# Gated attention scores kept in rows: masking by a TensorE bias, and one joint transposition of both attentions' probabilities

## The chip, the cores and the metric

The kernel runs on one core of a Trainium2 chip. The metric is the device time of one execution in microseconds (us), as the median of several executions. TensorE (PE in the rows) multiplies and transposes into PSUM; VectorE (DVE), ScalarE (ACT) and GpSimd (POOL) do the elementwise work; SyncE (SP) issues the DMAs.

## The reference, cut to what matters

One transformer layer over x of 2 x 1024 rows of 512. Its attention has 32 query heads over 8 key heads (4 query heads share a key head), head size 128, and is the mean of two attentions: a gated linear one (a scan with a decaying state) and a softmax over a sliding window of 64 positions.

```python
def step(S, x):
    q_t, k_t, v_t, g_t = x
    S = S * jnp.exp(g_t)[..., None] + k_t[..., None] * v_t[..., None, :]
    return (S, jnp.einsum('bhk,bhkv->bhv', q_t, S))
...
o_lin = gla_scan(softmax(q), softmax(k), v, log_sigmoid(g) / GATE_NORM)   # g = k before the softmax
y = sliding_window_attn(rope(q), rope(k), v)    # W = 64: the block of 64 and the one before it, masked, softmax
o_ = 0.5 * y + 0.5 * o_lin
x = x + _layernorm(_L0_attn_ref(_layernorm(x), ...))
x = x + _layernorm(_L0_ffn_ref(_layernorm(x), ...))   # NF4 quantised weights, silu(gate) * up, w3
```

## The kernel before

The attention part goes through 128 turns: 8 key heads times 16 tiles of 128 positions. A turn handles one tile for one key head, hence 4 query heads, hence tensors of 128 x 512. Turns are unrolled by four, as a step of a hardware loop (32 steps); the position in the step is `t.p`, 0 to 3. Every engine runs its own `turn(t)`, whose stages work on tile `t`, on the one before (`l1`), two before (`l2`) and three before (`l3`), and waits on counters (`wait_tile`) for the others. The order of work on each engine is that in which its `turn` is written. Nothing is reordered by a scheduler.

The gated attention of a tile is done in chunks. `gla_scores` (TensorE, tile `l2`) multiplies the scaled queries `qtT` (which VectorE writes last in a turn, in `gla_q`, semaphore `qt_d`) with the scaled keys `ktT` into PSUM bank X1, with keys on the partitions. `mask_gla` (VectorE) multiplies X1 by a 0/1 causal mask into `am`. The softmax probabilities of the window, `pr`, have queries on the partitions; `probabilities` (TensorE) transposes them into the same bank X1 once `am` is out, and `add_gla` (VectorE) adds X1 and `am` into `pa`. `output` multiplies `pa` with the values.

Names that the prediction uses, with their engine and line: `qtT` (VectorE L587, the last work of a turn but for the dequantisation in turn 0), `am` (VectorE L615), `kt` (VectorE L579, the keys' softmax times decay), `gh`, `kneg` and `gl` (VectorE L554, L555, L560: logarithm of the decay in two halves, functions `log_decay` and `low_decay`), `su` and `sr` (VectorE L627, L638: the state), `pa` (VectorE L621), `pmx`/`npm` (VectorE L601, L604: maxima of the window's scores, function `p_max`, which waits for `sc_done` of `scores` on TensorE, L883 and L891), `rp` (VectorE L610, reciprocal of the softmax sums), `qrT` (ScalarE L428, a copy out of PSUM that `scores` needs). Beside the attention, VectorE and GpSimd dequantise the second part's weights: VectorE writes fifteen terms `f_s` (L676) for each step, in portions of 2, 4, 5 and 4 over the four turns, and GpSimd adds them up in `f_acc` (L343) one turn later, so in portions of 4 (turn 0), 1 (turn 1), 4 (turn 2) and 5 (turn 3).

In this text "turn 2" is a turn with `t.p` of 2, and likewise turn 0, 1 and 3.

Of the kernel before, what the change touches and what calls it, by code (L numbers as in the profile page):

```python
# [34 lines left out]
P = 128  # L35
# [106 lines left out]
def attention(nc, sem, bank, rows, xh, xl, ident, stats, x_rows, wq_v, wk_v, wv_v, wo_v, wf_v, wf_p, dq_v, dq_p,  # L142
              cosc, sinc, winmask, causal, cumsum, identc, keepc):

    with ExitStack() as ctx:
        def sb(name, shape, dt=F32):
# [10 lines left out]
        cau = sb("cau", [P, 512])  # L157
# [13 lines left out]
        qtT = sb("qtT", [P, 2, GRP, 2, WIN])  # L171
        pr = sb("pr", [P, 2, 512])
        am = sb("am", [P, 512])
# [46 lines left out]
            rp_d am_d pa_d su_d em_d sr_d acc_d qrope_p krope_p qn_p pn_p  # L220
# [22 lines left out]
        def _(sp):  # L243
# [33 lines left out]
            for dst, src in ((cos[:], cosc), (sin[:], sinc), (f_s[:, 0:2, :], winmask), (cau[:], causal), (cum[:], cumsum),  # L277
                             (keep[:], keepc)):
                sp.dma_start(dst, src).then_inc(s["consts"], 16)
# [104 lines left out]
        def _(act):  # L384
# [56 lines left out]

            def copy_ktT(t):
# [34 lines left out]
            def turn(t):  # L477
                l1, l3 = t.back(1), t.back(3)
                if l3.real():
                    copy_o(l3)  # L480
                if l1.real():
                    q_exps(l1)
                    decays(l1)
                if t.real():
                    k_exps(t)
                    nf4_abs(t)
                if l1.real():
                    copy_qrT(l1)
# [35 lines left out]
        def _(dve):  # L524
# [57 lines left out]
            def gla_q(t):  # L582
# [107 lines left out]
            def turn(t):  # L690
# [7 lines left out]
                if l2.real():  # L698
                    mask_gla(l2)
# [96 lines left out]
            nc.vector.tensor_copy(win[:], f_s[:, 0:2, :]).then_inc(s["z_id"], 1)  # L796
            nc.vector.tensor_copy(cumh[:], cum[:]).then_inc(s["z_id"], 1)
# [620 lines left out]
```

## Time and profile before

| | |
|---|---|
| median of 3 runs | 2118.87 us (2117.91 to 2120.97) |
| span of the profiled execution | 2121.1 us |
| busy share of the span: TensorE | 89% |
| VectorE | 81% |
| ScalarE | 53% |
| GpSimd | 61% |
| one step (4 turns) in the middle of the attention part | 51.55 us |

For the profiled execution the profile gives its span, and no other time; the span stands 2.2 us above the median of the runs, which is 0.1%. The attention part takes about the first 1730 us. The shares of the whole span mix it with the last part, in which TensorE works nearly alone, so the rows further down come from the steady stretch in the middle.

### The profile page before, as it was taken

The numbers are of one execution on the slowest core, as the hardware profiler recorded it, in microseconds if no ns is written. First come the engines' busy times: TensorE is split into PE (matmuls) and PEld (weight loads), VectorE is DVE, ScalarE is ACT, GpSimd is POOL, SyncE is SP. The second block draws the span as 40 slices with busy tenths as digits, with TensorE's granted clock in tenths as the row PEclk, the third lists the DMA queues.
The fourth block names the chain that finished last, engine by engine and source line by source line (L and its number), as shares of the span: only waits on it lengthen the run. The fifth ranks groups of instructions, "written<-read, shape, count | busy, mean of one in ns | idle before, by whom it ended". The sixth has DMA issues, their size and how long they took to land. (4 is left out here: it accounts for less than half of the span.)

```text
span 2121.1 us, 41545 instructions
## 1 busy us (share of the span) xinstructions
PE 1893.0 (89%) x10676; PEld 1170.7 (55%) x10676; DVE 1724.4 (81%) x4335; ACT 1122.9 (53%) x4514; POOL 1292.9 (61%) x1189
## 2 busy tenths in 40 slices
PE   3799999998899999999999999998999869999998
PEld 2455555555555555555555555555555535544443
DVE  6899999999999999999999999999999964412022
ACT  6555555555555555555555555555555545512121
POOL 4777777767776677777777777777777724112111
PEclk8999999999999999999999999999999979999999
DMA  5000000000000000000000000000000033100000
GB/s 177 22 23 22 22 22 22 22 24 26 27 22 22 22 22 22 22 22 22 22 22 22 22 22 24 28 22 22 22 22 22 15 110 100 36 21 20 0 20 20
DMA packets 47051, 63.85 MB, mean 30 GB/s; under 512 B 5232, under 2 KB 20080, under 8 KB 47024
## 3 DMA queue, kind: packets, MB, share of 16 engines
q1 hardware_dynamic: 47024, 63.52, 9.3%
q8 instruction: 13, 0.21, 0.0%
q14 instruction: 14, 0.11, 0.0%
HBM read 50.86 MB, written 12.65 MB: 30 GB/s over the span
## 5 line engine op out<-in xcount | busy, mean ns | idle before, releaser
L343 POOL TENSOR_TENSOR f_acc<-f_acc,f_s 128x512 f32<-128x512 f32 x416 | 552.6, 1328 | 26.1 <-POOL f_acc L343 0.5
L437 ACT ACTIVATE pr<-bank,npm 128x128 f32<-128x128 f32 x512 | 180.9, 366 | 402.1 <-DVE npm L604 402.1
L864 PE MATMUL bank<-wh,xh 128*128 (+1 forms) x1024 | 335.2, 327 | 4.0 <-POOL wl L331 4.0
L864 PE MATMUL bank<-wl,xh 128*128 (+1 forms) x1024 | 335.0, 327 | 0.0
L864 PE MATMUL bank<-wh,xl 128*128 (+1 forms) x1024 | 334.7, 327 | 0.0
L325 POOL TENSOR_TENSOR pr<-pr,rp 128x512 f32<-128x512 f32 x128 | 133.1, 1039 | 257.4 <-DVE rp L610 257.4
L409 ACT ACTIVATE qe<-bank,nqm 128x128 f32<-128x128 f32 x512 | 180.9, 365 | 189.2 <-DVE qs L536 189.2
L676 DVE TENSOR_SCALAR f_s<-f_nrm 128x512 f32<-128x512 f32 x480 | 243.1, 568 | 4.4
L1349 POOL TENSOR_TENSOR hl<-hf,hh 128x512 f16<-128x512 f32 (+1 forms) x44 | 50.8, 1154 | 288.2 <-ACT hh L1218 288.2
L307 POOL TENSOR_TENSOR qc<-qc,qs 128x512 f32<-128x512 f32 x128 | 162.7, 1271 | 75.9 <-DVE qs L536 75.6
L1287 DVE SCALAR_TENSOR_TENSOR hf<-bank,sg 128x512 f32<-128x512 f32 (+1 forms) x44 | 30.4, 690 | 218.4 <-PE bank L1137 206.8
L853 PE MATMUL bank<-wh,oT 128*128 (+1 forms) x512 | 194.3, 380 | 4.1 <-ACT oT L473 2.5
L853 PE MATMUL bank<-wl,oT 128*128 (+1 forms) x512 | 194.0, 379 | 0.0
L842 PE MATMUL bank<-qtT,ktT 128*128 128x512 f32 x256 | 137.5, 619 | 29.9 <-DVE qtT L587 29.9
L318 POOL TENSOR_TENSOR qe<-qe,rq 128x512 f32<-128x512 f32 x128 | 147.3, 1151 | 0.5 <-DVE rq L596 0.5
L1137 PE MATMUL bank<-xh,w12h 128*128 (+3 forms) x352 | 135.3, 384 | 2.6 <-DVE xl L1244 1.4
L864 PEld LDWEIGHTS bank<-wh,xl 128*128 (+1 forms) x1024 | 100.6, 98 | 67.1 <-issue 1.1
L864 PEld LDWEIGHTS bank<-wl,xh 128*128 (+1 forms) x1024 | 100.6, 98 | 66.6 <-issue 0.6
L891 PEld LDWEIGHTS bank<-krT,qrT 128*128 128x128 f32 x1024 | 135.0, 192 | 3.6
L891 PE MATMUL bank<-krT,qrT 128*128 128x128 f32 x1024 | 135.6, 275 | 0.0
L1137 PE MATMUL bank<-xl,w12h 128*128 (+3 forms) x352 | 135.4, 385 | 0.0
L1137 PE MATMUL bank<-xh,w12l 128*128 (+3 forms) x352 | 135.2, 384 | 0.0
(176 smaller groups left out, 5017.2 us busy)
## 6 DMA issues: line engine op xcount, KB each, us to landing
raw_qkv<-wq SPq DMA_DIRECT2D x36, 256.0 KB, 2.3
raw_o<-wo SPq DMA_DIRECT2D x36, 256.0 KB, 2.6
f_raw<-wf SPq DMA_DIRECT2D x33, 256.0 KB, 2.6
dequantised<-f_dq SPq DMA_DIRECT2D x32, 256.0 KB, 2.0
wt<-dequantised SPq DMA_DIRECT2D x31, 256.0 KB, 3.1
rows<-x SPq DMA_DIRECT2D x4, 1024.0 KB, 8.7
xr<-x SPq DMA_DIRECT2D x16, 256.0 KB, 5.2
out<-yo SPq DMA_DIRECT2D x16, 256.0 KB, 2.0
```

What stands on the lines that cost most here:

```text
L307: nc.gpsimd.tensor_tensor(qc[:, r, :], qc[:, r, :], qs[:, r, :], ALU.add).then_inc(s["qrope_p"], 1)
L318: nc.gpsimd.tensor_tensor(v, v, rq[:, r, :].unsqueeze(2).to_broadcast([P, GRP, P]), ALU.mult).then_inc(s["qn_p"], 1)
L325: nc.gpsimd.tensor_tensor(v, v, rp[:, r, :].unsqueeze(2).to_broadcast([P, GRP, P]), ALU.mult).then_inc(s["pn_p"], 1)
L343: nc.gpsimd.tensor_tensor(f_acc[:], f_acc[:], f_s[:, k % 8, :], ALU.add).then_inc(s["f_ad"], 1)
L409: last = nc.scalar.activation(qe[:, r, h * P:(h + 1) * P], PQ[:, h * P:(h + 1) * P], ACT.Exp, bias=nqm[:, r, h:h + 1], scale=1.0 / WSCALE, ...
L437: last = nc.scalar.activation(pr[:, r, j * P:(j + 1) * P], SC[:, j * P:(j + 1) * P], ACT.Exp, bias=npm[:, r, j:j + 1], scale=ATT_SCALE, ac ...
L676: nc.vector.tensor_scalar(f_s[:, k % 8, :], f_nrm[:], float(BOUND[k]), float(DELTA[k]), ALU.is_gt, ALU.mult).then_inc(s["f_sd"], 1)
L842: nc.tensor.matmul(X1[:], ktT[:, r, :], qtT[:, r].rearrange("p h b n -> p b h n"), start=True, stop=True).then_inc(s["at_done"], 1)
L853: last = nc.tensor.matmul(PW[:], oT[:, t.p % 2, h].rearrange("p b n -> p (b n)"), w[:, sl + h, QW + KVW:WW], start=(h == 0 and k == 0), st ...
L864: last = nc.tensor.matmul(dst, av, w[:, sl + c, lo:hi], start=(n == 0), stop=(n == 3 * NC - 1))
L891: last = nc.tensor.matmul(SC[:, j * P:(j + 1) * P], qrT[:, r, b, 2 * hp:2 * hp + 2, :].rearrange("p h n -> p (h n)"), keys, start=False, s ...
L1137: last = nc.tensor.matmul(dst[0:n, :], ww[:, d, off + c * P:off + c * P + n], x4, start=(k == 0), stop=(k == 3 * NC - 1))
```

## The change

Five things change at once.

1. `gla_scores` swaps its operands, so the gated scores come out with queries on the partitions, as `pr` has them. Instead of one product of 512 columns there are four (two of 64 key columns, two of 128). Ahead of them two bfloat16 products with the identity add a bias `cau`, 0 where a key is allowed and -3e38 where it isn't.
2. `mask_gla` and `add_gla` go. A new `merge` on VectorE takes the maximum of X1 and 0 and adds it to `pr`, in place, over 128 and then 256 columns. The 128 columns left of the 512 can hold no gated score.
3. `probabilities` transposes that sum, and ScalarE copies it out of X1 into `pa` (`copy_pa`).
4. On ScalarE `copy_qrT` moves ahead of `k_exps`. On VectorE `log_decay` moves from before `state` to behind `p_max`.
5. `qtT` is laid out by window block first, then head; the mask is converted to bfloat16 once at the start.

```diff
@@ scalar
+            def copy_pa(t):
+                wait_tile(act, s["pt_done"], t)
+                wait_tile(act, s["o_done"], t, 2)
+                nc.scalar.activation(pa[:, t.p % 2, :], X1[:], ACT.Copy).then_inc(s["pa_ev"], 1)
@@ scalar turn
                 if l1.real():
                     q_exps(l1)
                     decays(l1)
+                    copy_qrT(l1)
                 if t.real():
                     k_exps(t)
                     nf4_abs(t)
+                if l2.real():
+                    copy_pa(l2)
                 if l1.real():
-                    copy_qrT(l1)
                     p_exps(l1)
@@ vector
-            def mask_gla(t):
+            def merge(t):
+
                 wait_tile(dve, s["at_done"], t)
-                wait_tile(dve, s["pa_d"], t, 1)
-                nc.vector.tensor_tensor(am[:], X1[:], cau[:], ALU.mult).then_inc(s["am_d"], 1)
-
-            def add_gla(t):
-                wait_tile(dve, s["pt_done"], t)
-                wait_tile(dve, s["am_d"], t)
-                wait_tile(dve, s["o_done"], t, 2)
-                nc.vector.tensor_tensor(pa[:, t.p % 2, :], X1[:], am[:], ALU.add).then_inc(s["pa_d"], 1)
+                wait_tile(dve, s["pn_p"], t)
+                v = pr[:, t.p % 2, :]
+                half = lambda a: a.rearrange("p (h n) -> p h n", h=GRP)[:, 0:2, 0:WIN]
+                nc.vector.scalar_tensor_tensor(out=half(v), in0=half(X1[:]), scalar=0.0, in1=half(v),
+                                               op0=ALU.max, op1=ALU.add)
+                nc.vector.scalar_tensor_tensor(out=v[:, 2 * P:], in0=X1[:, 2 * P:], scalar=0.0, in1=v[:, 2 * P:],
+                                               op0=ALU.max, op1=ALU.add).then_inc(s["pm_d"], 1)
@@ vector turn
                 if l2.real():
-                    mask_gla(l2)
+                    merge(l2)
                 if l1.real():
                     gla_k(l1)
                 if l3.real():
                     add_out(l3)
-                if t.real():
-                    log_decay(t)
                 if l2.real():
                     state(l2)
-                    add_gla(l2)
                 if l1.real():
                     p_max(l1)
                 if t.real():
+                    log_decay(t)
                     low_decay(t)
@@ tensor, gla_scores
-                wait_tile(pe, s["pa_d"], t, 1)
-                nc.tensor.matmul(X1[:], ktT[:, r, :], qtT[:, r].rearrange("p h b n -> p b h n"),
-                                 start=True, stop=True).then_inc(s["at_done"], 1)
+                wait_tile(pe, s["pa_ev"], t, 1)
+                half = lambda a: a.rearrange("p (h n) -> p h n", h=GRP)[:, 0:2, 0:WIN]
+                nc.tensor.matmul(half(X1[:]), identb[:], half(cau[:]), start=True, stop=False)
+                nc.tensor.matmul(X1[:, 2 * P:], identb[:], cau[:, 2 * P:], start=False, stop=False)
+                for b in range(2):
+
+                    keys = (b + 1) * WIN
+                    for hp in range(2):
+                        j = 2 * b + hp
+                        last = nc.tensor.matmul(X1[:, j * P:j * P + keys],
+                                                qtT[:, r, b, 2 * hp:2 * hp + 2, :].rearrange("p h n -> p (h n)"),
+                                                ktT[:, r, 0:keys], start=False, stop=(j == 3))
+                last.then_inc(s["at_done"], 1)
@@ tensor, probabilities
-                wait_tile(pe, s["pn_p"], t)
-                wait_tile(pe, s["am_d"], t)
+                wait_tile(pe, s["pm_d"], t)
```

On VectorE, a turn from the masking to the last half of the decay stood so before (a name ahead of the arrow is what is written, "bank" is PSUM, `rows` the running output):

```order
L615 TENSOR_TENSOR am<-bank,cau 128x512 [waits s_pa_d,s_at_done]
L575 RECIPROCAL rks<-ksum 128x1 [waits s_ke_ev]
L579 SCALAR_TENSOR_TENSOR kt<-ke,rks,ked 128x128 [waits s_u_done,s_dec_ev,s_rks_d]
L646 TENSOR_TENSOR rows<-bank,rows 128x512 [waits s_wo_done,s_zeroed]
L554 TENSOR_TENSOR gh<-kneg,kabs 128x128 [waits s_small_done,s_kneg_d,s_l1_ev]
L555 TENSOR_TENSOR kneg<-kneg,kabs 128x128
L627 TENSOR_TENSOR su<-bank,sr 128x128 [waits s_u_done]
L638 TENSOR_SCALAR sr<-su,edT 128x128 [waits s_su_d,s_dec_ev]
L621 TENSOR_TENSOR pa<-bank,am 128x512 [waits s_am_d,s_pt_done]
L601 TENSOR_REDUCE pmx<-bank 128x4 [waits s_sc_done]
L604 TENSOR_SCALAR npm<-pmx 128x4 [waits s_pmx_d]
L560 TENSOR_TENSOR gl<-kneg,gh 128x128 [waits s_g_d]
```

and so in the changed kernel:

```order
L625 SCALAR_TENSOR_TENSOR pr<-bank,pr 128x2x64 [waits s_pn_p,s_at_done]
L627 SCALAR_TENSOR_TENSOR pr<-bank,pr 128x256
L581 RECIPROCAL rks<-ksum 128x1 [waits s_ke_ev]
L585 SCALAR_TENSOR_TENSOR kt<-ke,rks,ked 128x128 [waits s_u_done,s_dec_ev,s_rks_d]
L653 TENSOR_TENSOR rows<-bank,rows 128x512 [waits s_wo_done,s_zeroed]
L634 TENSOR_TENSOR su<-bank,sr 128x128 [waits s_u_done]
L645 TENSOR_SCALAR sr<-su,edT 128x128 [waits s_su_d,s_dec_ev]
L608 TENSOR_REDUCE pmx<-bank 128x4 [waits s_sc_done]
L611 TENSOR_SCALAR npm<-pmx 128x4 [waits s_pmx_d]
L560 TENSOR_TENSOR gh<-kneg,kabs 128x128 [waits s_small_done,s_kneg_d,s_l1_ev]
L561 TENSOR_TENSOR kneg<-kneg,kabs 128x128
L566 TENSOR_TENSOR gl<-kneg,gh 128x128 [waits s_g_d]
```

The 128 x 512 multiplication and addition are gone, two shorter operations stand at the head, and `gh` and `kneg`, which stood between `kt` and `su`, now stand directly ahead of `gl`, with the wait for TensorE's scores (`s_sc_done`) ahead of all three.

On ScalarE, the same turn's work from the copies of the rotated keys to the first exponentials of the window was, before:

```order
L420 ACTIVATE ked<-bank 128x128
L423 ACTIVATE edT<-bank 128x130 [waits s_sr_d,s_qt_d]
L391 ACTIVATE va<-bank 128x128 [waits s_o_done,s_krope_d,s_kv_done]
L392 ACTIVATE vm<-bank 64x128
L393 ACTIVATE vm<-bank 64x128
L396 ACTIVATE ke,ksum<-bank,nkm 128x128 [waits s_nkm_d]
L398 ACTIVATE kabs<-bank 128x128
L400 ACTIVATE kabs<-kabs 128x128 [waits s_kabs_ev]
L402 ACTIVATE kabs<-kabs 128x128 [waits s_e1_ev]
L428 ACTIVATE qrT<-bank 128x4x2x64 [waits s_sc_done,s_qrT_done]
L437 ACTIVATE pr,psm<-bank,npm 128x128 [waits s_pt_done,s_npm_d]
L437 ACTIVATE pr,psm<-bank,npm 128x128 x3
```

and is now:

```order
L419 ACTIVATE ked<-bank 128x128
L422 ACTIVATE edT<-bank 128x130 [waits s_sr_d,s_qt_d]
L427 ACTIVATE qrT<-bank 128x4x2x64 [waits s_sc_done,s_qrT_done]
L390 ACTIVATE va<-bank 128x128 [waits s_o_done,s_krope_d,s_kv_done]
L391 ACTIVATE vm<-bank 64x128
L392 ACTIVATE vm<-bank 64x128
L395 ACTIVATE ke,ksum<-bank,nkm 128x128 [waits s_nkm_d]
L397 ACTIVATE kabs<-bank 128x128
L399 ACTIVATE kabs<-kabs 128x128 [waits s_kabs_ev]
L401 ACTIVATE kabs<-kabs 128x128 [waits s_e1_ev]
L444 ACTIVATE pa<-bank 128x512 [waits s_pt_done]
L436 ACTIVATE pr,psm<-bank,npm 128x128 [waits s_pt_done,s_npm_d]
```

The copy `qrT` moved ahead of seven instructions, and the new copy `pa` stands between them and the exponentials.

On TensorE, the path from the gated scores to the scores of the window was, before (`bank<-qtT,ktT` are the gated scores, `bank<-ident,qc` and `bank<-ident,pr` transpositions, `bank<-krT,qrT` the scores of the window):

```order
L842 MATMUL bank<-qtT,ktT 128x512 [waits s_pa_d,s_ktT_ev,s_qt_d]
L834 MATMUL bank<-ident,qc 128x128 [waits s_qt_d,s_qrope_p]
L834 MATMUL bank<-ident,qc 128x128 x3
L908 MATMUL bank<-qtT,sr 128x512 [waits s_oT_ev,s_sr_d]
L911 MATMUL bank<-va,kt 128x128 [waits s_dec_ev]
L901 MATMUL bank<-ident,pr 128x128 [waits s_am_d,s_pn_p]
L901 MATMUL bank<-ident,pr 128x128 x3
```

and is now:

```order
L849 MATMUL bank<-cau,identb 128x2x64 [waits s_pa_ev,s_ktT_ev,s_qt_d]
L850 MATMUL bank<-cau,identb 128x256
L856 MATMUL bank<-ktT,qtT 128x64 x2
L856 MATMUL bank<-ktT,qtT 128x128 x2
L840 MATMUL bank<-ident,qc 128x128 [waits s_qt_d,s_qrope_p]
L840 MATMUL bank<-ident,qc 128x128 x3
L923 MATMUL bank<-qtT,sr 128x512 [waits s_oT_ev,s_sr_d]
L926 MATMUL bank<-va,kt 128x128 [waits s_dec_ev]
L916 MATMUL bank<-ident,pr 128x128 [waits s_pm_d]
L916 MATMUL bank<-ident,pr 128x128 x3
```

One product became six; the rest of the row keeps its order, and the transposition (`bank<-ident,pr`) waits for `merge` in place of `am` and the normalised `pr`.

## Rows read from the trace of the kernel before

**Rows 1.** The page's head: the span of the profiled execution.
```profile
span 2121.1 us, 41545 instructions
```

**Rows 2.** Stretch 400 to 600 us: busy PE, PEld, DVE, ACT, POOL; PE clock, DMA.
```profile
400.00:600.00 200.00, 181.12 (x1073) 118.16 (x1072) 190.05 (x483) 116.02 (x512) 143.50 (x132) 1.00 0.07 22
```

**Rows 3.** Timeline of VectorE in turn 2: start, us, instruction, idle before.
```profile
1002.53 0.68 DVE L587 TENSOR_TENSOR qtT<-bank,edT 128x512 f32<-128x512 f32 x1
...
1005.21 0.69 DVE L615 TENSOR_TENSOR am<-bank,cau 128x512 f32<-128x512 f32 x1 [0.85 <-PE bank L842]
...
1006.00 1.03 DVE L579 SCALAR_TENSOR_TENSOR kt<-ke,rks,ked 128x128 f32<-128x128 f32 x1
...
1007.55 0.82 DVE L554 TENSOR_TENSOR gh<-kneg,kabs 128x128 f16<-128x128 f32 x1
1008.30 0.28 DVE L555 TENSOR_TENSOR kneg<-kneg,kabs 128x128 f32<-128x128 f32 x1
...
1008.89 0.90 DVE L638 TENSOR_SCALAR sr<-su,edT 128x128 f32<-128x128 f32 x1
...
1010.31 0.67 DVE L601 TENSOR_REDUCE pmx<-bank 128x4 f32<-128x512 f32 x1
...
1011.10 0.28 DVE L560 TENSOR_TENSOR gl<-kneg,gh 128x128 f16<-128x128 f32 x1
1011.30 1.76 DVE L676 TENSOR_SCALAR f_s<-f_nrm 128x512 f32<-128x512 f32 x5
```

**Rows 4.** Timeline of GpSimd in turn 2: its four additions, then two alone.
```profile
1005.61 5.44 POOL L343 TENSOR_TENSOR f_acc<-f_acc,f_s 128x512 f32<-128x512 f32 x4
...
1006.96 1.27 POOL L343 TENSOR_TENSOR f_acc<-f_acc,f_s 128x512 f32<-128x512 f32 x1
...
1008.31 1.39 POOL L343 TENSOR_TENSOR f_acc<-f_acc,f_s 128x512 f32<-128x512 f32 x1
```

**Rows 5.** Timeline of VectorE and GpSimd in turn 3.
```profile
1015.47 0.68 DVE L587 TENSOR_TENSOR qtT<-bank,edT 128x512 f32<-128x512 f32 x1
...
1018.55 7.03 POOL L343 TENSOR_TENSOR f_acc<-f_acc,f_s 128x512 f32<-128x512 f32 x5
...
1022.95 3.58 DVE L676 TENSOR_SCALAR f_s<-f_nrm 128x512 f32<-128x512 f32 x4
```

**Rows 6.** Timeline of turn 0: the score path on TensorE, and what surrounds it.
```profile
1028.94 0.67 DVE L587 TENSOR_TENSOR qtT<-bank,edT 128x512 f32<-128x512 f32 x1
...
1029.67 1.12 PE L842 MATMUL bank<-qtT,ktT 128*128 128x512 f32 x2 [0.90 <-DVE qtT L587]
...
1032.15 0.60 PE L901 MATMUL bank<-ident,pr 128*128 128x128 f32 x4
...
1033.44 0.58 ACT L428 ACTIVATE qrT<-bank 128x512 f32<-128x512 f32 x1
...
1034.12 0.38 PE L883 MATMUL bank<-win,identb 128*128 128x512 bf16 x1 [1.37 <-issue]
...
1034.34 1.05 PE L891 MATMUL bank<-krT,qrT 128*128 128x128 f32 x8
...
1037.28 0.52 DVE L655 SCALAR_TENSOR_TENSOR f_safe<-f_max 128x8 f32 x1
...
1033.57 1.40 POOL L343 TENSOR_TENSOR f_acc<-f_acc,f_s 128x512 f32<-128x512 f32 x1
```

**Rows 7.** Timeline of turn 1: masking, the transposition, the last small subtraction.
```profile
1045.33 0.68 DVE L615 TENSOR_TENSOR am<-bank,cau 128x512 f32<-128x512 f32 x1
...
1046.16 0.63 PE L901 MATMUL bank<-ident,pr 128*128 128x128 f32 x4 [1.02 <-DVE am L615]
...
1049.91 0.28 DVE L560 TENSOR_TENSOR gl<-kneg,gh 128x128 f16<-128x128 f32 x1
```

**Rows 8.** Groups by line: count, busy us, mean ns, idle before and its cause.
```profile
L615 DVE TENSOR_TENSOR am<-bank,cau 128x512 f32<-128x512 f32 x128 | 88.1, 688 | 29.3 <-PE bank L842 27.1
...
L1287 DVE SCALAR_TENSOR_TENSOR hf<-bank,sg 128x512 f32<-128x512 f32 x40 | 27.6, 691 | 195.2 <-PE bank L1137 183.6 <-issue 11.5
```

More of the change, by code:

```diff
@@ L156, in attention @@
         identb = sb("identb", [P, P], BF16)
-        cau = sb("cau", [P, 512])
+        cau = sb("cau", [P, 512], BF16)
         cum = sb("cum", [P, 130])
@@ L170, in attention @@
         qrT = sb("qrT", [P, 2, 2, GRP, WIN])
-        qtT = sb("qtT", [P, 2, GRP, 2, WIN])
+        qtT = sb("qtT", [P, 2, 2, GRP, WIN])
         pr = sb("pr", [P, 2, 512])
-        am = sb("am", [P, 512])
         pa = sb("pa", [P, 2, 512])
@@ L276, in _ @@
             load_weights(1, 0, 1)
-            for dst, src in ((cos[:], cosc), (sin[:], sinc), (f_s[:, 0:2, :], winmask), (cau[:], causal), (cum[:], cumsum),
+            for dst, src in ((cos[:], cosc), (sin[:], sinc), (f_s[:, 0:2, :], winmask), (f_s[:, 2, :], causal), (cum[:], cumsum),
                              (keep[:], keepc)):
@@ L477, in turn @@
             def turn(t):
-                l1, l3 = t.back(1), t.back(3)
+                l1, l2, l3 = t.back(1), t.back(2), t.back(3)
                 if l3.real():
@@ L586, in gla_q @@
                 wait_tile(dve, s["o_done"], t, 2)
-                nc.vector.tensor_tensor(qtT[:, r].rearrange("p h b n -> p h (b n)"),
-                                        X0[:].rearrange("p (h n) -> p h n", h=GRP),
-                                        edT[:, r, 0:P].unsqueeze(1).to_broadcast([P, GRP, P]), ALU.mult)\
+                nc.vector.tensor_tensor(qtT[:, r].rearrange("p b h n -> p h b n"),
+                                        X0[:].rearrange("p (h b n) -> p h b n", h=GRP, b=2),
+                                        edT[:, r, 0:P].rearrange("p (b n) -> p b n", b=2).unsqueeze(1)
+                                        .to_broadcast([P, GRP, 2, WIN]), ALU.mult)\
                     .then_inc(s["qt_d"], 1)
@@ L796, in _ @@
             nc.vector.tensor_copy(win[:], f_s[:, 0:2, :]).then_inc(s["z_id"], 1)
+            nc.vector.tensor_copy(cau[:], f_s[:, 2, :]).then_inc(s["z_id"], 1)
             nc.vector.tensor_copy(cumh[:], cum[:]).then_inc(s["z_id"], 1)
             nc.vector.memset(krT[:], 0.0).then_inc(s["z_id"], 1)
-            dve.wait_ge(s["z_id"], 5)
+            dve.wait_ge(s["z_id"], 6)
             turns(dve, 3, turn)
@@ L814, in _ @@
             pe.wait_ge(s["consts"], 96)
-            pe.wait_ge(s["z_id"], 5)
+            pe.wait_ge(s["z_id"], 6)
             slot = lambda t: (t.i // NC) % 2 * NC
@@ L907, in inter_and_update @@
                 wait_tile(pe, s["oT_ev"], t, 1)
-                nc.tensor.matmul(PO[:], sr[:, r, :], qtT[:, r].rearrange("p h b n -> p b h n"), start=True, stop=False)
+                nc.tensor.matmul(PO[:], sr[:, r, :], qtT[:, r].rearrange("p b h n -> p (b h n)"), start=True, stop=False)
                 if t.back(-1).real():
@@ L925, in output @@
                 r = t.p % 2
-                wait_tile(pe, s["pa_d"], t)
+                wait_tile(pe, s["pa_ev"], t)
                 wait_tile(pe, s["v_ev"], t)
@@ L1383, in constants @@
     win = np.ascontiguousarray(win.reshape(P, 2, 512))
+    n = np.arange(P)[:, None] % WIN
+    cau = np.zeros((P, 2, 2, P), np.float32)
+    for b in range(2):
+        cau[:, b] = np.where(n + b * WIN >= slot, 0.0, -3e38)[:, None, :]
+    cau = np.ascontiguousarray(cau.reshape(P, 512))
     j = np.arange(P)[:, None]
     i = np.arange(P)[None, :]
-    cau = (j <= i).astype(np.float32).reshape(P, 2, 1, WIN)
-    cau = np.ascontiguousarray(np.broadcast_to(cau, (P, 2, GRP, WIN)).reshape(P, 512))
     mid = P // 2 - 1
```

2 lines of the change are left out of this document (1 added, 1 removed).

## The prediction

> **What bounds the kernel now.** The span is 2121.1 us, 2.2 us above the median of the runs [rows 1]. I read the stretches first, because the whole span mixes two kinds of work. In the steady 200 us of the attention part VectorE is busy for 190.05 us, TensorE for 181.12, GpSimd for 143.50 and ScalarE for 116.02, at a granted TensorE clock of 1.00, the 2.4 GHz level, and a DMA share of 0.07 [rows 2]. So VectorE is the bound, and TensorE is close behind. No transfer is in the way, and the change moves none but the mask's, once, at the start.
>
> But 190 us busy is not 190 us of work, and that decides this case. In the timeline of VectorE `gh` takes 0.82 us while the equally wide `kneg` right behind it takes 0.28 [rows 3]. `gh` ends at 1008.37, and an addition on GpSimd ends at 1008.23 (1006.96 + 1.27). `sr` takes 0.90 us and ends at 1009.79; the next addition ends at 1009.70 (1008.31 + 1.39) [rows 3, 4]. `kt`, 1.03 us, ends at 1007.03, beside the addition's end at about 1006.9. All three have no PSUM operand. `am`, which reads PSUM, lies over GpSimd's work just the same and has its usual 0.69 us in all turns [rows 3, 8]. I read this as a rule of the trace: a VectorE instruction whose tensors all lie in SBUF, issued while GpSimd runs one, is held until that one has ended. One that gets in ahead of GpSimd's next addition goes through (`kneg` starts at 1008.30, the addition at 1008.31, and that addition then lasts 1.39 us in place of 1.27). The additions come every 1.36 us or so with 0.08 us between them.
>
> The Trainium skill (GPSIMD Engine Reference, Key points) says that GpSimd shares its SBUF interfaces with VectorE and that they contend where VectorE has two SBUF inputs or is in a two-port mode. The trace agrees: 0.82 us against 0.28.
>
> **The simple sum.** Per turn VectorE loses `am` and `pa`, two operations of 128 x 512 with a mean of 0.688 us [rows 8]. Start to start such an operation costs about 0.60 us (the next starts 0.08 before the end), so 1.20 us. `merge` has 128 and 256 columns. The same kind of instruction out of PSUM takes 0.691 us for 512 columns [rows 8], and 128 columns take 0.28 [rows 3], so 1.07 ns a column: 0.28 and 0.42 us, less the overlap 0.20 + 0.33 = 0.53 us. `merge` reads PSUM and isn't held. That is 0.67 us less in a turn and 86 us less in 128. I don't forecast this, because what is freed runs into GpSimd's additions. I go through the four turns of a step. Time 0 of a turn is the end of `qtT`: 1003.21 in turn 2, 1016.15 in turn 3, 1029.61 in turn 0 [rows 3, 5, 6]. GpSimd's schedule hangs on VectorE's early work of the turn, which stays, so its additions keep their places relative to 0.
>
> **The score path on TensorE** comes first, since in the new order `gh`, `kneg` and `gl` stand behind `pmx`. In turn 0 the gated scores start at 0.06 and the transposition 2.48 us later (1029.67 to 1032.15). Four transpositions take 0.44, the window bias 0.22, the eight passes of the scores 1.05: ready at 4.25, if no wait lies between. One does now: L883 starts at 1034.12, 1.37 us idle, right after the copy `qrT` has ended (1033.44 + 0.58) [rows 6]. Moving the copy takes that wait away. It can then start at about 1.8 and is over at 2.4, before L883 is due at 3.0. What is behind it on ScalarE (`va` to `kabs`) slips by about 1 us, and the first who needs it is `gh`, which itself moved back to 5.2. The copy `pa` costs what `qrT` does, 0.58 us, right behind `kabs`. ScalarE, busy 58% of the stretch [rows 2], waits there for the maxima anyway. If it did not, each late tenth would delay `rp`.
>
> What do the new products cost? Bias: 384 columns at the pace of the 512-column one (0.22 us [rows 6]), 0.16 us. Four products of two passes: 128 columns take 0.13 us a pass at most (1.05/8), at most 1.05 us together; if the 64-column ones cost half, 0.75 or so. The old product took 0.96 us until its successor in turn 0 started, so the difference lies between -0.06 and +0.16 us. I take +0.13, near the upper end, because in the rows the passes come at one pace that a weight load also has to fit in.
> By the Trainium skill (TensorE: Matmul & The Clock Gate, LDWEIGHTS) a load takes its number of columns at 1.2 GHz, 107 ns for 128, which no 64-column pass could hide; the sum by it would be +0.16 us. No row here has a 64-column pass.
>
> So scores are ready at 4.38, `pmx` starts at 4.42, and `gh` 0.79 us later (1010.31 to 1011.10 in the old order [rows 3]), at 5.2. VectorE itself could be at `pmx` by 3.8 (`merge` from 1.24 to 1.8, `kt` held to 2.5, output sum, `su`, `sr` held to 3.75), so it will now wait about 0.6 us for the scores.
>
> **Turn 1** has a single addition on GpSimd, early. `am` starts at 1045.33 and the transposition at 1046.16, 0.15 after `am` is out; `gl` starts at 1049.91 [rows 7]. New: `merge` ends at 1045.93, transposition 1046.08, scores 1.71 us later, `pmx` 1047.83, `gh` 1048.62, `kneg` +0.20, `gl` 1049.14. Gain 0.77 us; I take 0.70, since the window bias of this turn reads its address from a register and may start later.
>
> **Turn 2.** `am` waited 0.85 us for TensorE, and still will (TensorE gains as much in turn 1 as VectorE does). Scores at 5.3, `gh` at 6.1. The additions end at 2.40 + 5.44 = 7.84. `gh` is held to the end of the third, 6.4; `kneg` slips in behind it; `gl` has to wait for `kneg`'s result, so it comes 0.32 us behind and is held to 7.84. The five `f_s` start at 7.90, before at 8.09 [rows 3, 4]. **Gain 0.19 us**, where 0.67 were freed.
>
> **Turn 3.** Five additions, until 1025.58. `gh` arrives at 5.2, just behind the start of the third (5.15), is held to 6.42, `kneg` passes, `gl` is held to 7.9, one `f_s` passes, one is held to each of the next ends, two are free. Last `f_s` at 10.45; before 10.38 (1022.95 + 3.58) [rows 5]. **Loss 0.07 us.**
>
> **Turn 0.** The second addition starts at 1033.57 and lasts 1.40 us; without `kneg` slipping in it lasts 1.27, so it ends at 5.23, and the third starts at 5.31 [rows 6]. `gh` at 5.20 just catches this end, `kneg` slips in, `gl` is held to 6.7, the block maximum follows, and `f_safe` is held to the end of the last addition, as it was (0.52 us for eight elements [rows 6]). The last addition ends 0.12 us earlier. **Gain 0.12 us.**
>
> Sum of a step: 0.70 + 0.19 - 0.07 + 0.12 = 0.94 us, times 32 steps 30 us: 2118.9 - 30 = **2089 us**. TensorE doesn't become the bound: it is idle for 18.9 us of the stretch's 200 [rows 2], so 4.9 us of a step of 51.55, and gets 0.5 us of work more.
>
> **The rivals.**
> *Turn 0 misses the end at 5.23.* `gh` comes there 0.03 us ahead by my sum, with an error of 0.1 or more. If it misses, `gl` is held to the last addition's end at 8.05 and the block maximum follows it: 0.71 us later than before. A step then gains 0.11 us: **2115 us**, chance 0.25.
> *The saving comes in full*: `gl` isn't held when it stands close behind `kneg`, or the queue slides so that it goes through. For: `kneg` was never held, and no row shows `gl` inside an addition. Against: `f_s` is held by the rows of turn 3, 3.58 us for four against 1.76 for five. The simple sum then holds, 86 us: **2033 us**, chance 0.17.
> *Slower.* The score path is 0.3 us later than I have it (slow small products, or ScalarE late with `qrT`). From 0.27 us on, `gh` in turn 2 (6.1 against 6.37) misses the third addition's end; `gl` follows at 8.4 and the `f_s` 0.5 us later than before. Turn 0 has lost 0.71, turn 3 0.07, turn 1 gains only 0.4. A step loses 0.9 us: 28 us, **2147 us**, chance 0.13. It speaks for it that `log_decay` was moved out of a place where it filled a wait of VectorE, and now stands behind one.
>
> **How the numbers follow.** The forecast has chance 0.45, with a range of its own of 2078 to 2102. The range of all reaches down to the full saving, a little below it, and up past the missed end with its own error: 2028 to 2124. Outside are the slower case and the tails. A measurement of this kernel can tell about 0.2%, 4 us, from no change. Faster by more: the forecast, the full saving and half of the missed end, 0.74. Within: the other half, 0.13. Slower: 0.13.
>
> **What would show it.** In the profile after: `merge` at 0.28 and 0.42 us; no idle time at the window bias; `pmx` waiting for the scores, 0.5 us or so in turns 0, 2 and 3; `gl` held for 1.0 us or more in turns 0, 2 and 3 and 0.28 us in turn 1; turns 2 and 3 nearly as long as before, turn 1 0.7 us shorter. Short `gl` everywhere would prove me wrong on the bound, a long `gh` with `gl` at the last addition in turn 0 on the timing, and waits of TensorE for `pr` or `pa` on both.

## The result, and the profile after

The changed kernel takes 2131.27 us (median of 4 runs, 2126.36 to 2135.44), the one before on the same chip 2119.15 (4 runs). The ratio is 1.0056, 95% interval 1.0037 to 1.0075: **slower by 0.6%**. Forecast were 2089 us, a range of 2028 to 2124, and a chance of 0.13 for slower. The time lies outside the range, on the other side of no change.

The profiled execution took 2127.6 us. Its page's head comes first, then stretches, with the columns of [rows 2].

```profile
span 2125.8 us, 43562 instructions
```

The stretches:

```profile
400.00:600.00 200.00, 182.33 (x1189) 128.73 (x1188) 183.71 (x481) 128.69 (x533) 143.31 (x132) 0.99 0.07 22
...
774.60:777.60 3.00, 3.00 (x11) 1.90 (x10) 2.25 (x7) 2.70 (x10) 2.92 (x3) 0.50 0.00 0
...
825.80:828.80 3.00, 3.00 (x10) 2.18 (x10) 2.06 (x8) 1.90 (x11) 2.68 (x3) 0.50 0.13 47
```

VectorE is busy for 183.71 us of the 200 in place of 190.05 [rows 2]. So work did go away, and the time did not fall. And the clock, 1.00 before, is 0.99 here. The last two rows show where that comes from: each is 3 us out of a stretch of 3.4 us at 0.50, the 1.2 GHz level. There are nine such stretches between 100 and 1660 us, eight in turn 0 and one (at 119 us) in turn 1. Before there was none from 80 to 1700 us.

VectorE's groups by line tell where the freed time went (the columns are those of [rows 8]).

```profile
L561 DVE TENSOR_TENSOR kneg<-kneg,kabs 128x128 f32<-128x128 f32 x128 | 95.0, 743 | 0.0
L566 DVE TENSOR_TENSOR gl<-kneg,gh 128x128 f16<-128x128 f32 x128 | 92.8, 725 | 4.4
...
L627 DVE SCALAR_TENSOR_TENSOR pr<-bank,pr 128x256 f32<-128x256 f32 x128 | 52.8, 412 | 0.0
L625 DVE SCALAR_TENSOR_TENSOR pr<-bank,pr 128x128 f32<-128x128 f32 x128 | 36.8, 288 | 50.3 <-PE bank L856 47.9
```

`merge` costs 288 + 412 ns, as forecast, in place of 688 (`am`) and 679 (`pa`). But `kneg` has a mean of 743 ns and `gl` of 725. In the trace of before the same groups were short:

```profile
L560 DVE TENSOR_TENSOR gl<-kneg,gh 128x128 f16<-128x128 f32 x128 | 36.5, 285 | 0.0
L555 DVE TENSOR_TENSOR kneg<-kneg,kabs 128x128 f32<-128x128 f32 x128 | 35.7, 279 | 0.0
```

That is 0.90 us more a turn, 116 us in 128 turns. Part of it is not new but moved: `sr`, held before (899 ns), now mostly gets through (393), and the means of `f_s` (568 to 490 ns, 480 of them) and `gh` (655 to 544) fell too, while that of `npm` rose (170 to 285).

The timeline of VectorE for the same kinds of turn as [rows 3, 5, 6, 7], in the order turn 2, 3, 0, 1 (start, us, instruction, idle before):

```profile
1004.37 0.67 DVE L593 TENSOR_TENSOR qtT<-bank,edT 128x512 f32<-128x512 f32 x1
...
1007.30 0.29 DVE L625 SCALAR_TENSOR_TENSOR pr<-bank,pr 128x128 f32<-128x128 f32 x1 [1.10 <-PE bank L856]
...
1011.09 0.37 DVE L611 TENSOR_SCALAR npm<-pmx 128x4 f32<-128x4 f32 x1
1011.37 0.28 DVE L560 TENSOR_TENSOR gh<-kneg,kabs 128x128 f16<-128x128 f32 x1
1011.57 1.35 DVE L561 TENSOR_TENSOR kneg<-kneg,kabs 128x128 f32<-128x128 f32 x1
1012.96 0.29 DVE L566 TENSOR_TENSOR gl<-kneg,gh 128x128 f16<-128x128 f32 x1
1013.16 1.76 DVE L683 TENSOR_SCALAR f_s<-f_nrm 128x512 f32<-128x512 f32 x5
...
1017.33 0.67 DVE L593 TENSOR_TENSOR qtT<-bank,edT 128x512 f32<-128x512 f32 x1
...
1023.23 1.34 DVE L560 TENSOR_TENSOR gh<-kneg,kabs 128x128 f16<-128x128 f32 x1
1024.50 0.28 DVE L561 TENSOR_TENSOR kneg<-kneg,kabs 128x128 f32<-128x128 f32 x1
1024.81 1.25 DVE L566 TENSOR_TENSOR gl<-kneg,gh 128x128 f16<-128x128 f32 x1
1025.98 2.50 DVE L683 TENSOR_SCALAR f_s<-f_nrm 128x512 f32<-128x512 f32 x4
...
1030.88 0.67 DVE L593 TENSOR_TENSOR qtT<-bank,edT 128x512 f32<-128x512 f32 x1
...
1035.95 0.69 DVE L608 TENSOR_REDUCE pmx<-bank 128x4 f32<-128x512 f32 x1 [0.40 <-PE bank L907]
...
1036.78 0.29 DVE L560 TENSOR_TENSOR gh<-kneg,kabs 128x128 f16<-128x128 f32 x1
1036.99 1.36 DVE L561 TENSOR_TENSOR kneg<-kneg,kabs 128x128 f32<-128x128 f32 x1
1038.38 1.32 DVE L566 TENSOR_TENSOR gl<-kneg,gh 128x128 f16<-128x128 f32 x1
1039.62 0.67 DVE L658 TENSOR_REDUCE f_max<-f_abs 128x512 f32 x1
...
1043.11 0.67 DVE L593 TENSOR_TENSOR qtT<-bank,edT 128x512 f32<-128x512 f32 x1
...
1048.10 0.41 DVE L627 SCALAR_TENSOR_TENSOR pr<-bank,pr 128x256 f32<-128x256 f32 x1
...
1051.82 0.29 DVE L566 TENSOR_TENSOR gl<-kneg,gh 128x128 f16<-128x128 f32 x1
```

GpSimd in that turn 0, its first two additions and the third (its timeline, same columns):

```profile
1034.11 2.68 POOL L342 TENSOR_TENSOR f_acc<-f_acc,f_s 128x512 f32<-128x512 f32 x2
...
1036.86 1.33 POOL L342 TENSOR_TENSOR f_acc<-f_acc,f_s 128x512 f32<-128x512 f32 x1
```

In turn 0 the second addition ends at 1036.79 and the third starts at 1036.86. `gh` is issued at 1036.78, right at the end of the second, so it isn't held (0.29 us). It also uses up the gap: `kneg` comes at 1036.99, inside the third addition, and is held to its end (1038.19), and `gl`, issued at 1038.38, is held to the end of the fourth (1039.55). In turn 2 `npm`, four elements wide, is itself held to the end of the third addition (1011.42), `gh`, issued right behind it, takes the gap, and `kneg` stands inside the fourth (GpSimd's third and fourth addition of that turn):

```profile
1010.16 1.26 POOL L342 TENSOR_TENSOR f_acc<-f_acc,f_s 128x512 f32<-128x512 f32 x1
...
1011.51 1.27 POOL L342 TENSOR_TENSOR f_acc<-f_acc,f_s 128x512 f32<-128x512 f32 x1
```

Turn 3 is as forecast. In turn 1 the only addition is over by then, and everything is short.

Lengths of the turns, from one end of `qtT` to the next, in undisturbed steps:

| us | turn 2 | turn 3 | turn 0 | turn 1 | step |
|---|---|---|---|---|---|
| before | 12.95 | 13.47 | 11.58 | 13.55 | 51.55 |
| forecast change | -0.19 | +0.07 | -0.12 | -0.70 | -0.94 |
| after | 12.95 | 13.56 | 12.22 | 12.76 | 51.50 |
| change | 0.00 | +0.09 | +0.64 | -0.79 | -0.05 |

So an undisturbed step is as long as before. On top of it nine of the 31 steps take 51.8 to 52.1 us: eight that hold a stretch at 0.50, and the one behind the stretch at 119 us. TensorE's timeline shows what happens there. The first row is from a disturbed turn 0, the others from an undisturbed turn 0 and the turn 1 behind it:

```profile
774.56 1.92 PE L923 MATMUL bank<-qtT,sr 128*128 128x512 f32 x2
...
1031.62 0.23 PE L849 MATMUL bank<-cau,identb 128*128 128x128 bf16 x1 [1.88 <-DVE qtT L593]
1031.68 0.27 PE L850 MATMUL bank<-cau,identb 128*128 128x256 bf16 x1
1031.79 1.06 PE L856 MATMUL bank<-ktT,qtT 128*128 128x64 f32 x8
1032.68 0.60 PE L840 MATMUL bank<-ident,qc 128*128 128x128 f32 x4
1033.12 1.02 PE L923 MATMUL bank<-qtT,sr 128*128 128x512 f32 x2
...
1034.20 0.60 PE L916 MATMUL bank<-ident,pr 128*128 128x128 f32 x4
...
1048.56 0.66 PE L916 MATMUL bank<-ident,pr 128*128 128x128 f32 x4 [1.98 <-DVE pr L627]
```

The same two products L923 take 1.02 us in the undisturbed turn and 1.92 where the clock is at 0.50. In such a turn 0 `npm` is held for 1.1 to 1.2 us, in an undisturbed one not at all (0.17).

TensorE stands still for 1.88 us ahead of turn 0, where it waits for `qtT`, and for 1.98 us in turn 1, where the transposition waits for `merge`. Before, its idle time stood in shorter pieces: at the window bias, behind the copy `qrT`, 0.85 us in turn 3 (the row below) and 1.37 in turn 0; ahead of turn 0 0.90; and in turn 1 1.02 and 0.41 [rows 6, 7].

```profile
1020.12 0.38 PE L883 MATMUL bank<-win,identb 128*128 128x512 bf16 x1 [0.85 <-issue]
```

The waits at the window bias are gone, as forecast, so TensorE reaches the waits that are left sooner. The transposition of turn 1 doesn't start later than it did (4.78 us behind the end of `qtT`, before 4.96); TensorE stands ready for it earlier.

The balance of the two profiled executions: between the first and the last `qtT` the changed kernel needs 7.6 us more. The nine disturbed steps have 4.1 of them, 21 undisturbed ones -0.9, the first step +1.8 (with stretches at 0.50 at 88 and 119 us), the last three turns +2.7 (with stretches at 1703 and 1713 us). The part before the first `qtT` and the tail give 2.9 back, which makes 4.7 us of span. In `after_again`, the same kernel run once more, the first step has no such stretch and takes 52.40 us in place of 54.48. By that and by the undisturbed steps the stretches cost this execution about 9 us, an estimate: 4.5 in the nine steps, 2.1 in the first, 2.7 at the end. Without them it would lie some 4 us below the kernel before, not 5 above.

### The profile page after: what moved, and what is told of

The parts are those of the page before. It is cut to its first block and busy times, and to the rows that moved or that the text cites. A ratio compares the mean times of both kernels' runs of the same rounds, so it can differ in the third digit from the quotient of the medians.

```text
span 2125.8 us, 43562 instructions
## 1 busy us (share of the span) xinstructions
PE 1906.8 (90%) x11700; PEld 1267.5 (60%) x11700; DVE 1674.8 (79%) x4336; ACT 1214.5 (57%) x4642; POOL 1285.5 (60%) x1189
## 5 line engine op out<-in xcount | busy, mean ns | idle before, releaser
L342 POOL TENSOR_TENSOR f_acc<-f_acc,f_s 128x512 f32<-128x512 f32 x416 | 545.8, 1312 | 26.1 <-POOL f_acc L342 0.5
L683 DVE TENSOR_SCALAR f_s<-f_nrm 128x512 f32<-128x512 f32 x480 | 206.1, 490 | 4.4
L923 PE MATMUL bank<-qtT,sr 128*128 128x512 f32 x256 | 139.1, 627 | 0.0
L856 PE MATMUL bank<-ktT,qtT 128*128 128x64 f32 (+1 forms) x1024 | 137.8, 278 | 0.0
L880 PEld LDWEIGHTS bank<-wh,xh 128*128 (+1 forms) x1024 | 101.0, 99 | 58.8 <-issue 6.1
```

Of the source, the lines that this page charges most:

```text
L342: nc.gpsimd.tensor_tensor(f_acc[:], f_acc[:], f_s[:, k % 8, :], ALU.add).then_inc(s["f_ad"], 1)
L683: nc.vector.tensor_scalar(f_s[:, k % 8, :], f_nrm[:], float(BOUND[k]), float(DELTA[k]), ALU.is_gt, ALU.mult).then_inc(s["f_sd"], 1)
L856: last = nc.tensor.matmul(X1[:, j * P:j * P + keys], qtT[:, r, b, 2 * hp:2 * hp + 2, :].rearrange("p h n -> p (h n)"), ktT[:, r, 0:keys], ...
L880: last = nc.tensor.matmul(dst, av, w[:, sl + c, lo:hi], start=(n == 0), stop=(n == 3 * NC - 1))
L923: nc.tensor.matmul(PO[:], sr[:, r, :], qtT[:, r].rearrange("p b h n -> p (b h n)"), start=True, stop=False)
```

## The experiments

The edits are against the changed kernel unless said otherwise. The ratios are against the kernel before, run beside them on the same chip, with medians of 2118.7, 2119.2 and 2120.9 us in the three groups.

### Where the logarithm of the decay stands

`decay_back` puts `log_decay` where it was, ahead of `state`:

```diff
+                if t.real():
+                    log_decay(t)
                 if l2.real():
                     state(l2)
                 if l1.real():
                     p_max(l1)
                 if t.real():
-                    log_decay(t)
                     low_decay(t)
```

> The changed kernel with log_decay put back ahead of state, where it stood before; copy_qrT stays where the change put it. In the changed kernel kabs is ready at 4.3 us of turns 3 and 0 and at 5.2 of turns 2 and 1, later than before (3.4), because the copy qrT now stands ahead. Theory H (what counts is at which end of a GpSimd addition the held VectorE instructions come out): gh waits for kabs, is held to the addition's end behind it, then sr and npm are held to later ends; turn 2 about 0.7 us longer than in the changed kernel, turn 0 0.2, turn 3 about as long, turn 1 0 to 0.3: 52.3 to 52.8 us a step instead of 51.5, 25 to 40 us slower than the changed kernel (2155 to 2170). Rival M (the loss comes only from log_decay having left a place where it filled a wait): 0.4 to 0.6 us a turn back, 50 to 70 us faster than the changed kernel.

Measured: 2177.69 us, ratio 1.0278 (1.0264 to 1.0292). VectorE in turn 0 (timeline):

```profile
1065.81 1.03 DVE L560 TENSOR_TENSOR gh<-kneg,kabs 128x128 f16<-128x128 f32 x1 [0.99 <-ACT kabs L401]
...
1067.35 0.91 DVE L645 TENSOR_SCALAR sr<-su,edT 128x128 f32<-128x128 f32 x1
1068.18 0.68 DVE L608 TENSOR_REDUCE pmx<-bank 128x4 f32<-128x512 f32 x1
```

With `copy_qrT` ahead on ScalarE `kabs` comes 1 us later, VectorE waits 0.99 us for it, `gh` and then `sr` are held, and the maxima come 2.3 us later than in the changed kernel (they start 6.70 us after the end of `qtT` in place of 4.39). So H holds in direction, with more loss than it gave (2155 to 2170 us): turn 0 is 0.60 us longer than in the changed kernel in place of 0.2, and there are 11 stretches at 0.50 between 100 and 1550 us. The rival M, 50 to 70 us faster, is out. Moving the copy made the other move necessary.

`decay_mid` puts it between `state` and `p_max`, so that it stands in the wait for the scores:

```diff
                 if l2.real():
                     state(l2)
+                if t.real():
+                    log_decay(t)
                 if l1.real():
                     p_max(l1)
                 if t.real():
-                    log_decay(t)
                     low_decay(t)
```

> The changed kernel with log_decay between state and p_max, so that gh and kneg use the time in which VectorE waits for TensorE's scores, and gl stands apart from them behind npm. Theory H: gh held to the second addition's end, kneg slips in, pmx, npm held to the third's, gl in the gap behind it: turn 0 shorter by 0.7 us than in the changed kernel, turn 3 by 0.3, turn 2 by 0.1, turn 1 the same: 50.4 us a step, 30 to 40 us faster than the changed kernel, 2095 to 2100. Rival M: 0.4 to 0.6 us a turn in all turns, so 50 to 70 us. Rival C (the whole loss is the granted clock): no more than a few us.

Measured: 2107.02 us, ratio 0.9938 (0.9924 to 0.9951), above the 2095 to 2100 expected. Undisturbed steps take 50.37 to 50.40 us, as forecast, but only 6 of 31 are undisturbed. The others take 51.2 to 51.9 (the first 52.4), with the clock at 0.50 in 17 stretches between 100 and 1700 us. Behind the first step the disturbed steps take 24 us more than undisturbed ones would, and the range was missed by 7.

### TensorE's order

`scores_first` lets the scores go ahead of the transposition that waits for `merge`, and `mid_scores_first` does both:

```diff
                 if l2.real():
                     inter_and_update(l2)
-                    probabilities(l2)
                 if l1.real():
                     scores(l1)
+                if l2.real():
+                    probabilities(l2)
```

> The changed kernel with scores(l1) ahead of probabilities(l2) on TensorE. It takes away the one long pause of TensorE (2.1 us in turn 1, waiting for merge) and brings the scores 0.44 us forward. Theory H: little on VectorE, because npm, gh, kneg and gl come out at the same ends of additions; turn 2 shorter by 0.15 us. Theory C (the dips of the granted clock in the steady part, absent before, come from that pause): no dips of 3.4 us between 100 and 1600 us, and the steps of 52.0 us gone, worth 6 to 13 us. Both: 2115 to 2122. If the dips stay, C is wrong and it is 2125 to 2132.

> decay_mid and scores_first together. Theory H: turn 2 then has its merge 0.9 us earlier and gains another 0.3 us: 49.8 to 50.2 us a step, 2075 to 2090 with no dips. If TensorE becomes the bound instead (47 us a step of work), still not above 50.5.

Measured: `scores_first` 2108.03 us, ratio 0.9947 (0.9933 to 0.9960), undisturbed steps 51.0 us. That is below both ranges given: the order gains 0.5 us a step (turn 2 0.27, turn 3 0.14, turn 0 0.07), where 0.15 was expected. The stretches at 0.50 stayed, 20 between 100 and 1700 us, in turn 0, so my theory that turn 1's stand-still alone makes them fell: that one had shrunk to 0.9 us, the one ahead of turn 0 was still 1.8.

`mid_scores_first` takes **2074.35 us**, ratio 0.9788 (0.9775 to 0.9802). That is just below the expected range of 2075 to 2090. Every step but the first is 50.14 to 50.18 us, and there is no stretch at 0.50 between 100 and 1670 us. It is the best version of all, 2.1% below the kernel before. Its undisturbed step is only 0.2 us shorter than that of `decay_mid`, 7 us in all; most of the 33 us between these two comes with the stretches that are gone. VectorE in turn 0 (timeline):

```profile
1057.14 1.04 DVE L560 TENSOR_TENSOR gh<-kneg,kabs 128x128 f16<-128x128 f32 x1 [0.34 <-ACT kabs L401]
1058.11 0.28 DVE L561 TENSOR_TENSOR kneg<-kneg,kabs 128x128 f32<-128x128 f32 x1
1058.31 0.68 DVE L608 TENSOR_REDUCE pmx<-bank 128x4 f32<-128x512 f32 x1
1059.02 0.52 DVE L611 TENSOR_SCALAR npm<-pmx 128x4 f32<-128x4 f32 x1
1059.45 0.28 DVE L566 TENSOR_TENSOR gl<-kneg,gh 128x128 f16<-128x128 f32 x1
```

Four instructions out of SBUF, but only two addition ends are waited for, since `pmx`, which reads PSUM, runs while GpSimd adds.

### The stretches at half the clock

`fill_pause` shortens the stand-still ahead of turn 0 by work of no use:

```diff
-                wait_tile(pe, s["qt_d"], t)
                 wait_tile(pe, s["ktT_ev"], t)
                 wait_tile(pe, s["pa_ev"], t, 1)
+                if t.p == 2:
+                    for _ in range(5):
+                        nc.tensor.matmul(X1[:], identb[:], win[:, 1, :], start=True, stop=True)
+                wait_tile(pe, s["qt_d"], t)
```

> The changed kernel with five extra bfloat16 products of 512 columns on TensorE at the end of turn 3, in front of the wait for qtT, where TensorE stands still for about 1.9 us; their result is overwritten. About 1.1 us of work in the pause, so nothing is delayed. Theory P (the clock dips come from this pause at the end of turn 3, 0.9 us before the change): no dips between 120 and 1650 us, all steps at 51.5 us, 5 to 12 us faster than the changed kernel run beside it. Rival: the dips come from the longer pause of turn 1 (2.1 us, untouched here) or from nothing of the kernel: they stay, and so does the time.

> The changed kernel itself, beside the others on the same chip: 2126 to 2136, with dips of the clock in the steady part.

Measured: `fill_pause` 2128.47 us, ratio 1.0049 (1.0036 to 1.0062); the changed kernel once more, `after_again`, 2134.83 us, ratio 1.0076 (1.0062 to 1.0090). None of the stretches stands in turn 0 any more, but six stand in turn 1, behind its stand-still of 1.9 us. The 6 us gained lie in the range expected, though the stretches didn't go and the filler itself costs 0.12 us in each turn 3 (undisturbed steps of 51.62 us). One of them in the view of stretches:

```profile
222.90:225.90 3.00, 3.00 (x11) 1.56 (x11) 2.60 (x10) 1.07 (x7) 0.34 (x1) 0.50 0.00 0
```

TensorE's waits between 80 and 1660 us in the changed kernel (us in total, times, longest us):

```profile
PE bank L849 <- DVE qtT L593: 81.5, 84, 1.9
PE bank L916 <- DVE pr L627: 56.3, 30, 2.0
```

and in `fill_pause`, where the wait for `qtT` is at most 1.4 us, in the first step (0.6 between 400 and 1600 us):

```profile
PE bank L919 <- DVE pr L627: 57.0, 30, 1.9
PE bank L852 <- DVE qtT L593: 43.6, 88, 1.4
```

Half the answer: the filler took away the stretches that its stand-still had made. So `scores_first_fill` shortens both, with the diffs of `scores_first` and `fill_pause` together:

> The changed kernel with the scores ahead of the transposition of the probabilities on TensorE (which shortens its stand-still in turn 1) and with five products of no use ahead of the wait for the queries at the end of turn 3 (which shorten the stand-still there). Each alone left stretches at half the granted clock. Theory C2 (a stand-still of TensorE of about 1.9 us, wherever it is, is followed by such a stretch): with both shortened there are none or nearly none in the attention part; every step takes the time of the undisturbed ones with the scores ahead, 51.0 us, so 2095 to 2104 us, a little below the 2108 us with the scores ahead alone. Rival (the stretches have a cause of their own, such as how busy TensorE is over longer times): they stay, 5 or more, in some turn, and the time stays at 2106 us or above.

Measured: 2103.03 us (2102.19 to 2103.12), ratio 0.9915 (0.9902 to 0.9929), as expected. Every step but the first is 51.0 to 51.1 us and no stretch at 0.50 stands between 70 and 1700 us. Its waits:

```profile
PE bank L852 <- DVE qtT L593: 69.0, 93, 1.1
PE bank L919 <- DVE pr L627: 24.8, 31, 0.8
```

All the runs fall into line with the longest stand-still of TensorE between 100 and 1550 us (the `short_adds` kernels and `before_reordered` follow further down):

| kernel | longest, us | stretches at 0.50, 100 to 1550 us |
|---|---|---|
| `after_short_adds` | 0.6 | 0 |
| `before_short_adds` | 0.9 | 0 |
| `mid_scores_first` | 1.0 | 0 |
| `scores_first_fill` | 1.0 | 0 |
| `before_reordered` | 1.2 | 0 |
| before | 1.4 | 0 |
| `scores_first` | 1.8 | 18 |
| `decay_mid` | 1.9 | 16 |
| `decay_back` | 1.9 | 11 |
| `fill_pause` | 1.9 | 6 |
| after | 2.0 | 7 |
| `after_again` | 2.0 | 6 |

Each of these stretches starts 0.1 to 1.5 us behind the end of a stand-still of 1.7 to 2.0 us. How busy TensorE is as a whole doesn't sort the kernels: in the 200 us from 400 it is busy for 181.12 us before, without a stretch, and for 182.33 after. The fillers shorten a stand-still and add work at once, so they alone can't tell the two apart; `mid_scores_first`, without fillers, has no stretch either.

### The additions on GpSimd

In these two GpSimd's repeated additions cover 64 of their 512 columns. The dequantised weights are therefore not those of the reference.

```diff
-nc.gpsimd.tensor_tensor(f_acc[:], f_acc[:], f_s[:, k % 8, :], ALU.add)
+nc.gpsimd.tensor_tensor(f_acc[:, 0:64], f_acc[:, 0:64], f_s[:, k % 8, 0:64], ALU.add)
```

> The kernel before with GpSimd's repeated additions f_acc over 64 columns in place of 512 (a seventh of the time or less each), so the dequantised weights are left wrong; all instructions, waits and VectorE operations are the same. Theory H (VectorE instructions without a PSUM operand are held until GpSimd's instruction ends): gh, kt, sr and f_s at their short times, 5 to 6 us less VectorE time in a step; TensorE becomes the bound at 46.5 to 47.5 us a step: 1960 to 2000. Rival (the long times are something else, and GpSimd is off the critical path): within 1% of 2119.

> The changed kernel with the same shortening. Theory H: kneg, gl and npm short everywhere, VectorE near 44 us of work a step, TensorE the bound with 0.1 us more work a turn but no wait for qrT: 46.5 to 47.5 us a step, within 1% of the kernel before with short additions. If the saved VectorE work counts in full: 0.67 us a turn, 86 us below it.

Measured: 1992.90 us for the kernel before (ratio 0.9401, 0.9387 to 0.9415) and 1968.32 for the changed one (0.9284, 0.9270 to 0.9297). The shape of the instructions on VectorE is untouched, yet `kneg` and `gl` fall to 0.28 and 0.29 us and `f_s` to 0.42. So what made them long are the additions. The steps are 47.61 and 46.82 us, and the difference is 24.6 us, 1.2% (just more than the 1% of theory H), not the 86 of the simple sum. The stretch of the changed one says why:

```profile
400.00:600.00 200.00, 197.56 (x1317) 142.02 (x1315) 171.03 (x535) 140.16 (x587) 102.52 (x146) 1.00 0.08 24
```

TensorE is busy for 197.56 us of 200. Without the holds TensorE is the bound in most turns. Turn 1 gets shorter by 0.77 us (12.77 against 13.54), turns 0 and 3 by 0.30 and 0.17, and turn 2 longer by 0.45.

### What the joined form is worth

`before_reordered` is the kernel before, with its masking and addition, in the order of the best version:

```diff
                     decays(l1)
+                    copy_qrT(l1)
                 if t.real():
                     k_exps(t)
                     nf4_abs(t)
                 if l1.real():
-                    copy_qrT(l1)
                     p_exps(l1)
...
-                if t.real():
-                    log_decay(t)
                 if l2.real():
                     state(l2)
-                    add_gla(l2)
+                if t.real():
+                    log_decay(t)
                 if l1.real():
                     p_max(l1)
+                if l2.real():
+                    add_gla(l2)
...
                     inter_and_update(l2)
-                    probabilities(l2)
                 if l1.real():
                     scores(l1)
+                if l2.real():
+                    probabilities(l2)
```

> The kernel before, with its masking, its addition and its 512-column product kept, but put in the order that did best for the changed kernel: the copy of the rotated queries moved ahead on ScalarE, TensorE's scores ahead of the transposition of the probabilities, and on VectorE the state, then the first half of the decay, then the maxima, then the addition, then the second half. It asks what the joining of the two attentions is worth when the order is the same. Theory H (VectorE's instructions out of SBUF are held until GpSimd's additions end, so an order is worth what it makes of those ends) says: VectorE has the masking and the addition of 512 columns each again, 0.67 us more in a turn than the joined form, and in this order the last operations of three turns fall one addition later or not at all: by my walk through the turns about 52.3 us a step, 2135 to 2150 us. Theory O (the order alone makes the gain, the joined form nothing): about as fast as the best version, 2070 to 2090 us. Between them, 2100 to 2130 us, both have a part.

Measured: 2133.38 us, ratio 1.0057 (1.0043 to 1.0070), every step but the first 51.9 us, just below the range of theory H. So the order alone gains nothing for the kernel before. In one and the same order the joined form takes 50.16 us a step and the old one 51.90: 1.74 us, times 32 steps 56 us, which is the 59 us between the two times. Of the 2.7 us of VectorE's work per step that the simple sum counts, two thirds arrive, once the order lets them.

## Why the prediction was wrong

**What held.** VectorE as the bound, the hold by GpSimd, the cost of `merge` (0.70 us), the new products (1.07 us until the successor against 0.96: +0.11, forecast +0.13), the scores' arrival (`pmx` at 4.40 in turn 0, forecast 4.42), turn 3 (+0.09 for +0.07), turn 1 (-0.79 for -0.70). The rule of the Trainium skill quoted there (GPSIMD Engine Reference, Key points) names two SBUF inputs or a two-port mode. `gh`, `kneg` and `gl` have two SBUF inputs and agree with it (0.28 us free, up to 1.38 held). `npm` has a single SBUF input of four elements and is held as well (0.17 us free, 0.37 in turn 2, up to 1.24 in a disturbed turn 0); whether it runs in such a mode no row shows.

Two sums on the new products were wrong, without effect on the forecast. With 1.05 us for the eight passes the upper bound of the difference is 0.16 + 1.05 - 0.96 = +0.25 us, not +0.16; with eight loads of the 107 ns quoted there it is 0.16 + 0.86 - 0.96 = +0.06. Measured is +0.11.

**The term that failed: turn 0**, a gain of 0.12 us forecast, a loss of 0.64 measured. The prediction put it as "`gh` at 5.20 just catches this end, `kneg` slips in". The times were right to 0.03 us (`gh` at 5.23, the end at 5.24, the next addition from 5.31), and that decided: `gh` came with the end itself, so it wasn't held, and took the gap that I had given to `kneg`. I had treated a gap as open to whatever is near. The rows show that it lets one instruction through: either the one behind a held one (turns 2 and 3), or one that arrives right then (turn 0), and the next is held for the whole addition. My rival "turn 0 misses the end" gave +0.71 for turn 0, by `gh` held and `gl` at the last end. Its place and nearly its price came true, by another pair of instructions.

**Turn 2**, -0.19 forecast, 0.00 measured: `npm` stood in no sum of mine as an instruction that can be held. It waited for the third end, `gh` took the gap, and `kneg` waited for the last. `gl`, for which the prediction named 1.0 us or more in this turn, went through (0.29).

These two alone, 0.76 and 0.19 us, take away the whole 0.94 us; with the small differences of turns 1 and 3 an undisturbed step is 0.05 us shorter than before, a time within 0.2% of before.

**What was in no rival: the granted clock.** I moved waits between engines and never asked how long TensorE stands still in one piece. With the waits for `qrT` gone, and only turn 1 shorter, TensorE's idle time gathered in two stand-stills of 1.9 to 2.0 us, with stretches at 1.2 GHz behind them. In the changed kernel each costs its step about 0.5 us, in `decay_mid` 24 us come to 1.4 a stretch. `scores_first_fill` against `scores_first` shows it with nearly the same schedule: 51.05 us in every step against 51.0 and 51.3 to 51.4 in turn, 5 us between the medians. So the missed gaps explain why nothing was gained, and the clock why it became slower. The forecast for slower (score path late, turn 2 misses) is not what happened: the score path was on time.

**What stays open.** Why only some of the equal stand-stills are followed by such a stretch (nine of 31 steps). Why in the changed kernel eight of the nine follow the shorter one (1.88 us, ahead of turn 0) is open too. The unprofiled executions of the changed kernel reach 2135 us at a mean clock of 0.969, against 0.975 in the profiled one, which fits more stretches, but no trace shows them.

## What to carry to other kernels

Where one engine holds another, freed time is worth what the next end of the holding engine makes of it: walk through the turns instruction by instruction, count every instruction that can be held (small ones too), and give each gap to one of them. Place instructions that can't be held (here those that read PSUM) between those that can. And after every reordering look at the longest single wait of TensorE, not only at its sum: here two more edits of order, at no cost in work, turned a loss of 0.6% into a gain of 2.1%.

## What was unexpected of the hardware

- A held instruction's length has nothing to do with its size: four elements (`npm`) took up to 1.24 us in the changed kernel instead of 0.17.
- With weights of its own for each, a pass of 64 columns in float32 cost TensorE what one of 128 does, 0.11 us from start to start.
- The granted clock fell to its lower level, for 3.4 us at a time, in a kernel whose TensorE is busy 91% of the stretch, after stand-stills of 1.7 to 2.0 us, and in none of the six kernels where they stayed at 1.4 or below.
